# A decoder kernel in which couplings move from VectorE to ScalarE, the router's pick goes by logits, and one scan and one decay stand earlier

## What is computed

```
x = norm(x + random_features(x))
x = norm(x + attention(x, ctx))
# three cycles: gf = sigmoid(net3(mean of x)), once; tf = sigmoid(net4(out)), per row
coupling = 0.1 + adaptive_range * (0.7 * gf + 0.3 * tf - 0.5) * 2.0
out = out + coupling * twist(out)          # x = norm(x + out)
# state space: h = a_t * h + x_conv**2, 16 states of each of 512 channels, summed over the states
x = norm(x + mamba(x))
x = norm(x + gelu(x @ ctx.T) * (x @ ctx.T) @ ctx)
probs = softmax(xt @ router_w + router_b)
gate, idx = max(probs), argmax(probs)      # the first of equal ones
x = norm(x + gate * (expert idx of 8)(x))
```

## Time and profile before

| | us |
|---|---|
| median of 3 runs | 3107.59 (3103.23 to 3112.39) |
| the profiled execution | 3099.29 |
| its span | 3097.5 |
| PE busy | 2540.1 (82%) |
| DVE busy | 2495.3 (81%) |
| ACT busy | 1727.8 (56%) |
| POOL busy | 1487.4 (48%) |

### The profile page before, as it was taken

The page is one execution under the profiler, slowest core; times in us unless marked ns, Lnnn a source line. Parts: engine busy times, 40 slices in busy tenths (PEclk is TensorE's granted clock), DMA queues, the critical chain, the costliest instruction groups (busy, mean ns, idle before and its releaser), DMA issues.

```text
span 3097.5 us, 41602 instructions
## 1 busy us (share of the span) xinstructions
PE 2540.1 (82%) x11020; PEld 1469.9 (47%) x11020; DVE 2495.3 (81%) x4288; ACT 1727.8 (56%) x3062; POOL 1487.4 (48%) x1159
## 2 busy tenths in 40 slices
PE   6896888979888897888988788888888889887556
PEld 3544554544444454445545444554544445454323
DVE  2368888897978889898888978788897888978783
ACT  1457564646657474665646466564656646465620
POOL 1046354554535455563545545354553545456460
PEclk7868888888989989999898899898898989978687
DMA  3000000000000000000000000000000000000000
GB/s 131 10 8 10 14 11 14 17 14 7 10 21 10 14 17 14 7 10 21 10 14 13 18 7 10 21 10 14 13 3 21 10 14 7 7 7 1 14 7 7
DMA packets 16849, 45.72 MB, mean 15 GB/s; under 512 B 2248, under 2 KB 7056, under 8 KB 16400
## 3 DMA queue, kind: packets, MB, share of 16 engines
q1 hardware_dynamic: 16656, 43.96, 4.2%
HBM read 35.57 MB, written 8.39 MB: 14 GB/s over the span
## 4 chain that ended last, share of the span: by engine, by line
PE 47%; DVE 28%; issue 14%; ACT 7%; DVEq 2%; POOL 1%; ACTq 0%; DMA 0%; SPq 0%; POOLq 0%
PE bank L535 45%; DVE h_ring L1087 14%; DVE x L1199 3%; DVE ln_stats L387 2%; DVE smax L991 1%; POOL ysum L1671 1%; ACT a_ring L1479 1%; DVE x L405 1%; DVE xpad L1093 1%; PE bank L413 1%; DVE soft L1066 1%; ACT L1485 1%; ACT L1339 1%; DVE ln_mv L391 1%; ACT spare L1420 1%
## 5 line engine op out<-in xcount | busy, mean ns | idle before, releaser
L1671 POOL TENSOR_TENSOR ysum<-ysum,h_ring 128x512 f32<-128x512 f32 x896 | 1155.2, 1289 | 633.3 <-DVE h_ring L1087 571.3
L1087 DVE TENSOR_TENSOR_SCAN h_ring<-a_ring,bank 128x512 f32<-128x512 f32 x1024 | 1172.7, 1200 | 27.2 <-ACT bank L1474 16.2
L1479 ACT ACTIVATE a_ring<-soft,decay 128x510 f32<-128x510 f32 x1024 | 675.7, 717 | 198.4 <-DVE h_ring L1087 198.0
L535 PE MATMUL bank<-w_expert_w,x45T 128*128 128x512 f32 x1024 | 541.1, 675 | 199.0 <-DVE x L1199 191.4
L535 PEld LDWEIGHTS bank<-w_expert_w,x45T 128*128 128x128 f32 x1024 | 213.2, 216 | 490.9 <-DVE x L1199 253.5
L1658 POOL TENSOR_TENSOR soft<-xc,soft 128x512 f32<-128x512 f32 x64 | 81.0, 1276 | 655.2 <-ACT soft L1457 655.2
L535 PE MATMUL bank<-x3T,w_winT 128*128 128x512 f32 x512 | 291.0, 704 | 39.7 <-ACT x3T L419 31.4
L991 DVE TENSOR_REDUCE smax<-bank 128x4 f32<-128x480 f32 x256 | 156.4, 652 | 143.1 <-PE bank L535 143.1
L535 PE MATMUL bank<-qT,kmask 32*120 32x256 f32 x1024 | 207.2, 497 | 50.2 <-ACT spare L1386 40.6
L535 PE MATMUL bank<-spare,w_cn_w 128*128 128x256 f32 x768 | 217.7, 408 | 37.0 <-ACT spare L1416 22.4
L1199 DVE SCALAR_TENSOR_TENSOR x<-bank,weight,x 128x256 f32<-128x256 f32 x512 | 212.5, 474 | 40.4 <-PE bank L535 40.4
(11 more groups left out here) (149 smaller groups left out, 3890.2 us busy)
## 6 DMA issues: line engine op xcount, KB each, us to landing
x0T<-in_xT SPq DMA_DIRECT2D x16, 512.0 KB, 3.3
x<-in_x SPq DMA_DIRECT2D x16, 512.0 KB, 4.3
out<-x SPq DMA_DIRECT2D x16, 512.0 KB, 3.0
ctxT<-in_ctxT SPq DMA_DIRECT2D x16, 240.0 KB, 2.5
ctxTb<-in_ctxT SPq DMA_DIRECT2D x16, 240.0 KB, 2.7
ctxb<-in_ctx SPq DMA_DIRECT2D x16, 240.0 KB, 3.0
w_expert_w<-in_expert_w SPq DMA_DIRECT2D x1, 2048.0 KB
w_winT<-in_winT SPq DMA_DIRECT2D x1, 1024.0 KB
```

The lines of the kernel that those rows point to most:

```text
L535: return pe.matmul(o, l, r, start=start, stop=stop)
L1087: scanned.then(v.tensor_tensor_scan(h_ring[:, k % HRING, :], a_ring[:, k % RING, :, :].rearrange("p b s -> p (b s)"), xc2, 0.0, ALU.mult, ...
L1479: a.activation(a_ring[:, k % RING, :, 1:S], delta[:, c, :].rearrange("p (b s) -> p b s", b=NB)[:, :, 1:S], ACT.Exp, scale=decay[:, k:k + 1 ...
L1671: p.tensor_tensor(out=total, in0=first, in1=h_ring[:, k % HRING, :], op=ALU.add)\
```

## The change

Three things. The coupling is made on ACT, as an Identity activation with the gate scale as scale and the base as bias, right behind the gate's tanh, and the base likewise on ACT behind the global network's tanh; DVE's `rotate` waits for the coupling. The expert is picked from the logits less their maximum (those equal to 0), in `route`, ahead of the exponential, and the weight is the reciprocal of the sum alone, since the largest term is 1. And in the order of the first cycle DVE's `states(m, 32)` becomes 33 and ACT's `decays(m, 36)` becomes 37, with the third square placed at k = 36 instead of 38.

```diff
-SQUARE_AT = (0, 18, 38, 59)
+SQUARE_AT = (0, 18, 36, 59)
...
-            def global_base(g):
-                v.wait_ge(glob_ready.sem, glob_ready.at(g, 3))
-                v.tensor_scalar(base[:, :], gt[:, :], glob_scale[:, :], base_sign[:, :], ALU.mult, ALU.add)\
-                    .then_inc(base_ready.sem, 1)
-                cyc_chain.start(v, g)
...
                 if s == 0:
-                    v.wait_ge(base_ready.sem, base_ready.at(g, 1))
-                v.wait_ge(gate_ready.sem, gate_ready.at(g, s + 1))
-                cyc_chain.link(v.tensor_scalar(couple[:, b, :], gate[:, b, :], gate_scale[:, :], base[:, b:b + 1],
-                                               ALU.mult, ALU.add))
+                    cyc_chain.start(v, g)
+                v.wait_ge(couple_ready.sem, couple_ready.at(g, s + 1))
...
+                v.wait_ge(logit_ready.sem, logit_ready.at(g, 1))
+                pick_chain.start(v, g)
+                pick_chain.link(v.scalar_tensor_tensor(out=prank[:, :, :], in0=logit[:, :, :], scalar=0.0,
+                                                       in1=over_tiles(row("rank")), op0=ALU.is_equal, op1=ALU.mult))
+                pick_chain.link(v.tensor_reduce(rmax[:, :], prank[:, :, :], AX, ALU.max))
+                pick_chain.then(v.tensor_tensor(out=pick[:, :, :], in0=prank[:, :, :], in1=over_experts(rmax[:, :]),
+                                                op=ALU.is_equal))
+
+            def weigh_expert(g):
+
                 v.wait_ge(prob_ready.sem, prob_ready.at(g, 1))
-                pick_chain.start(v, g)
-                pick_chain.then(v.tensor_reduce(pmax[:, :], prob[:, :, :], AX, ALU.max))
                 pick_chain.link(v.tensor_reduce(psm[:, :], prob[:, :, :], AX, ALU.add))
-                pick_chain.then(v.reciprocal(pinv[:, :], psm[:, :]))
-                pick_chain.link(v.tensor_tensor(out=pick[:, :, :], in0=prob[:, :, :], in1=over_experts(pmax[:, :]),
-                                                op=ALU.is_equal))
-                pick_chain.then(v.tensor_tensor(out=pgate[:, :], in0=pmax[:, :], in1=pinv[:, :], op=ALU.mult))
-                pick_chain.link(v.tensor_tensor(out=prank[:, :, :], in0=pick[:, :, :], in1=over_tiles(row("rank")),
-                                                op=ALU.mult))
-                pick_chain.link(v.tensor_reduce(rmax[:, :], prank[:, :, :], AX, ALU.max))
-                pick_chain.link(v.tensor_tensor(out=pick[:, :, :], in0=prank[:, :, :], in1=over_experts(rmax[:, :]),
-                                                op=ALU.is_equal))
+                pick_chain.link(v.reciprocal(pinv[:, :], psm[:, :]))
                 pick_chain.end()
-                v.tensor_tensor(out=weight[:, :, :], in0=pick[:, :, :], in1=over_experts(pgate[:, :]),
+                v.tensor_tensor(out=weight[:, :, :], in0=pick[:, :, :], in1=over_experts(pinv[:, :]),
                                 op=ALU.mult).then_inc(weight_ready.sem, 1)
...
-                states(m, 32)
-                if f is not None:
-                    global_base(f)
+                states(m, 33)
+                if f is not None:
                     rotate(f, 0)
                     rotate(f, 1)
                 states(m, 34)
...
+                    a.wait_ge(glob_ready.sem, glob_ready.at(g, 3))
+                    a.activation(base[:, :], gt[:, :], ACT.Identity, bias=base_sign[:, :], scale=glob_scale[:, :])\
+                        .then_inc(base_ready.sem, 1)
...
                     a.activation(gate[:, b, :], bank[b][:, 0:S], ACT.Tanh, bias=half_b4[:, :], scale=0.5)\
                         .then_inc(gate_ready.sem, 1)
+                    if s == 0:
+                        a.wait_ge(base_ready.sem, base_ready.at(g, 1))
+                    a.wait_ge(gate_ready.sem, gate_ready.at(g, s + 1))
+                    a.activation(couple[:, b, :], gate[:, b, :], ACT.Identity, bias=base[:, b:b + 1],
+                                 scale=gate_scale[:, :]).then_inc(couple_ready.sem, 1)
...
-                decays(m, 36)
+                decays(m, 37)
                 if f is not None:
                     cycle(f, 0)
                     nat()
```

More of the change, by code:

```diff
@@ L245, in program @@
         prob = sb("prob", [P, NT, EXPERTS])
-        pmax = sb("pmax", [P, NT])
         psm = sb("psm", [P, NT])
         pinv = sb("pinv", [P, NT])
-        pgate = sb("pgate", [P, NT])
         pick = sb("pick", [P, NT, EXPERTS])
@@ L337, in program @@
         gate_ready = sem("gate_ready", CYC)
-        cyc_chain = chain("cyc_chain", 3 * CYC)
+        couple_ready = sem("couple_ready", CYC)
+        cyc_chain = chain("cyc_chain", 2 * CYC)
         z_ready = sem("z_ready", 2 * CYC)
@@ L364, in program @@
         prob_ready = sem("prob_ready", 1)
-        pick_chain = chain("pick_chain", 8)
+        pick_chain = chain("pick_chain", 5)
         weight_ready = sem("weight_ready", 1)
@@ L1154, in route @@
                                 op=ALU.subtract).then_inc(logit_ready.sem, 1)
-            def pick_expert(g):
+                v.wait_ge(logit_ready.sem, logit_ready.at(g, 1))
[6 more added lines that the diff above has]
+            def weigh_expert(g):
                 v.wait_ge(prob_ready.sem, prob_ready.at(g, 1))
-                pick_chain.start(v, g)
-                pick_chain.then(v.tensor_reduce(pmax[:, :], prob[:, :, :], AX, ALU.max))
                 pick_chain.link(v.tensor_reduce(psm[:, :], prob[:, :, :], AX, ALU.add))
-                pick_chain.then(v.reciprocal(pinv[:, :], psm[:, :]))
-                pick_chain.link(v.tensor_tensor(out=pick[:, :, :], in0=prob[:, :, :], in1=over_experts(pmax[:, :]),
-                                                op=ALU.is_equal))
-                pick_chain.then(v.tensor_tensor(out=pgate[:, :], in0=pmax[:, :], in1=pinv[:, :], op=ALU.mult))
-                pick_chain.link(v.tensor_tensor(out=prank[:, :, :], in0=pick[:, :, :], in1=over_tiles(row("rank")),
-                                                op=ALU.mult))
-                pick_chain.link(v.tensor_reduce(rmax[:, :], prank[:, :, :], AX, ALU.max))
-                pick_chain.link(v.tensor_tensor(out=pick[:, :, :], in0=prank[:, :, :], in1=over_experts(rmax[:, :]),
-                                                op=ALU.is_equal))
+                pick_chain.link(v.reciprocal(pinv[:, :], psm[:, :]))
                 pick_chain.end()
-                v.tensor_tensor(out=weight[:, :, :], in0=pick[:, :, :], in1=over_experts(pgate[:, :]),
+                v.tensor_tensor(out=weight[:, :, :], in0=pick[:, :, :], in1=over_experts(pinv[:, :]),
                                 op=ALU.mult).then_inc(weight_ready.sem, 1)
@@ L1256, in turn_ @@
                 if b is not None:
-                    pick_expert(b)
+                    weigh_expert(b)
                 states(m, 22)
```

## The result

| | before | after |
|---|---|---|
| median of the runs, us | 3109.05 (4 runs) | 3176.39 (4 runs, 3167.32 to 3200.83) |
| ratio to before | | 1.0254, 95% interval 1.0223 to 1.0284 |
| span of the profiled execution | 3097.5 | 3176.4 |
| DVE busy | 2495.3 | 2418.8 |
| ACT busy | 1727.8 | 1787.0 |

DVE has 76 us less to do, and the kernel takes 67 us more by the medians and 79 us by the profiled spans. The forecast was 3212, with a range of 3172 to 3240. The sign and the place were right; the size of two terms was not, one in each direction. The ratios in this document and their intervals are the ones on record; they are not the quotients of the medians beside them (here 1.0217) and differ from these by up to 0.4%.

A forecast was written before the change was run, and what follows sets the result against it. No one engine bounds all; the path runs from ACT's table load through the network and PE's experts to DVE's combine. 13 turns at 7.4 us (96) plus other turns sum to +104, on 3107.6 giving 3212 us, range 3172 to 3240.

The forecast's parts named there:

- The hold: ACT waits for DVE's scan of step 33 before the third square, so the gelu table load starts 7.68 us later.
- The chain behind it: From the gelu table's end on ACT to the first gate: 5.49 us at full clock instead of 6.25, a gain of 0.76.
- TensorE's clock: PE idles between layers 1 and 2, so layers 2 to 4 run at the lower clock: 1.46 us more.
- Who waits: Experts 4 and 5 on PE end 8.38 us later; one combine goes ahead (0.39), so DVE's combine comes 8.0 later.
- The couplings: Moved from DVE to ACT, six a turn: only the second pair of rotations gains, 0.45 us in a turn.
- DVE's wait for the square goes under the wait for the experts: DVE's 0.88 us wait for ACT's square goes, but is hidden under its wait for PE's experts.
- The pick: DVE gains about 2 us in expert picking, but PE is late behind it: only 0.19 a turn comes through.
- The rest: Turns outside the 13 loop turns: turn 1 adds 3.5 us, turn 15 5.5, the last two -1, turn 0 no hold.
- Rival 2: Only DVE's own path counts, as if the experts were in time: 3184 or 3165 us; chance 0.07.
- Rival 1: PE's clock stays up, or comes back before it matters: 3192 us; chance 0.2.
- Rival 4: Faster, without ACT's hold: DVE's savings are left, 3098 or 3031 us; chance 0.03 faster, 0.03 for the edge.
- 3: Rival: low clock also covers keys and experts, and `route` delays the softmax: +2 us a turn, 3238; chance 0.08.

## Why the prediction held, and where it failed

*The hold:* predicted 7.68 later for the table load, measured 7.66. The step is right, in its place and in its size, and so is the reading of the plan (step 33). ACT's idle time is 6.44 for "about 6.4".

*The chain behind it:* 5.49 at full clock predicted; 5.50 with PE kept busy. Right.

*TensorE's clock:* this term was mis-sized. I took 1.46 from turn 1, where PE idles 7.03 us ahead of the same matmuls; measured are 2.54. I had read the granted clock of turn 1 from 271 to 276 only and took what the matmuls lost there for the price of the whole chain. Turn 1 of the kernel before, and turn 8 after (the granted clock is the third number from the end):

```profile
269.89:276.72 6.83, 3.45 (x8) 2.82 (x9) 6.83 (x8) 4.51 (x8) 6.05 (x6) 0.50 0.00 0
276.72:279.48 2.76, 2.50 (x10) 1.47 (x10) 1.20 (x2) 1.82 (x4) 2.47 (x3) 1.00 0.00 0
```

```profile
1560.65:1570.89 10.24, 7.16 (x18) 4.82 (x18) 0.00 (x0) 6.35 (x15) 2.52 (x2) 0.50 0.00 0
```

In turn 1 the clock was back after 3.45 of the 6.21 us of these matmuls. Here it stays low for 6.85 of the 7.64 us from layer 2's start to layer 4's end (1564.04 to 1571.68, for 5.03 before). Why it comes back later here isn't shown; the chains differ, as in the first cycle the global network's small matmuls stand between the layers. My upper end of 1.8 was too low too.

*Who waits:* the combine's shift was to be 8.0; the fourth stretch is 9.04 longer, which is 8.0 and the clock's 1.08 more. One product ahead of the others (0.4) is as predicted, and so is PE, not DVE's own path, as what is late. DVE's idle time ahead of the first rotation was to be 8 to 10 and is 12.22 in turn 8: my own numbers give 10.6 (1511.74 to 1521.28 + 1.05), and the rest is the clock's higher price.

*The couplings:* 0.45 in the second pair, nothing in the first and the third: measured -0.45 in the fifth stretch. Right in the changed kernel. One instruction takes 0.60 on ACT instead of the 0.55 I took. But the step "DVE's wait for the square goes under the wait for the experts" holds only with the square moved; without that the couplings cost 0.78. That is the cover that I named and didn't price.

*The pick:* this step failed. I predicted that 0.19 of about 2 us comes through, since PE idled only 0.19 us for DVE in turn 8, and I had turn 8 stand for all. Turn 9 of the same profile of the kernel before:

```profile
1666.73 0.60 PE L783 MATMUL bank<-w_ident,weight 128*8 128x128 f32 x4
1671.15 6.19 PE L535 MATMUL bank<-w_wo,qT 128*128 128x256 f32 x16 [3.81 <-DVE qT L1014]
```

PE idles 3.81 us for DVE there and the product behind it runs at the lower clock, 6.19 for 3.72. In ten of the 13 loop turns that idle time is 1.77 us or more; in three, turn 8 among them, it is about 0.2. In the changed kernel ten of 13 have none. The third stretch of turn 8 and that of turn 10, as rows of a stretch, say what sets turn 8 apart:

```profile
1472.27:1493.70 21.43, 21.24 (x116) 11.44 (x109) 19.84 (x34) 12.99 (x24) 16.20 (x13) 0.70 0.00 1
1840.32:1861.78 21.46, 15.17 (x108) 9.11 (x109) 19.76 (x34) 12.87 (x24) 16.22 (x13) 1.00 0.00 1
```

Both are as long. In turn 8 TensorE had the lower clock for much of the stretch, was busy nearly throughout and so as late as DVE; in turn 10, at the full clock, it idled 3.81 us for DVE. The three turns with 0.2 of idle time are those with a granted clock of 0.70 to 0.72. In the changed kernel a stretch at 0.70 or 0.71 takes 20.9 to 21.0 us, the two at 1.00 take 18.87: the same pick gives 0.5 where TensorE is slow and 2.6 where it isn't. DVE's own saving, from the logits to the scan behind the weights, is 2.2 in the mean (5.6 for 7.8), near the "about 2" of the prediction; what failed is how much of it PE would hide. So the saving comes through: 2.0 in a turn, of which 0.6 is the three products that ran at the lower clock before and don't after, and 19 us between the medians with the pick alone.

*The rest:* turn 15 was to add 5.5 and takes 0.7 off. Its hold is there (ACT idles 6.12 us for DVE's scan, and from norm 2's copies on ACT to the combine of experts 4 and 5 it is 26.5 for 19.9); what makes the rest of that turn 7.3 shorter I didn't work out. The last two turns give 3.9 for the 1 taken; turns 0 and 1 add 4.1 for 3.5. By the sum: 9.04 - 0.45 - 2.00 - 0.48 (small stretches) = 6.11 for my 7.4, and the median ended 36 below the forecast, near the low end. The terms make 25 of that (79 for 104); the other 10 is the scale, as the profiled execution lay 8.3 below its median before and 1.8 above it after. Too small a clock term hid part of the error in the pick. That the time lies in the range is in part luck. Rival 2 (only DVE's own path), at 3184 the nearest in its number, is false: the combine waits for PE's experts. Rival 1 (the clock stays up), at 3192, is false too: layers 2 to 4 run at the lower clock. Rival 4 is false; 3 was right in that the low clock costs more, but keys and experts take as long as before (1.78 and 3.60).

## What to carry to other kernels

Before an instruction is moved ahead of a block on an in-order engine, read what it waits for, and when that comes: here one square and one decay, 1.3 us of work, held the network for 7.7 us in every turn and made the kernel 2.5% slower than before; with the same piece behind the block it is about 1% faster than before, which is about what the pick gives alone. Count an idle time over all turns before one turn stands for them, above all where TensorE's clock differs between turns: an engine at half its clock hides another's lateness. A saving on one engine is worth what is late behind it, and moved work pushes back what stands behind it on its new engine: with the old schedule the couplings took 0.45 us off DVE in one stretch and made another 0.78 longer, by a later square.

## What the runs showed of the hardware

- The price of PE's idle time. Behind 6.84 us without a matmul, layer 2 took 2.08 us for 1.13; with matmuls of no use in that gap it took 1.13. The Trainium skill ("TensorE: Matmul & The Clock Gate", Part 1) has activity release the throttle; this pair of rows agrees.
- The same kernel, profiled twice, had turns of 178.68 and 180.41 us in the mean. The fourth and the fifth stretch agree within 0.01 us; the third and the last are 0.35 and 1.50 longer in the second profile, with 3.6 to 3.8 us more at the lower clock in each. Its two medians, 3057 and 3072, lie 15 us apart, on two chips.
- A tiny instruction of DVE with two SBUF inputs can last until POOL's instruction ends. The old comparison (L1162, 128x32) took 1.23 to 1.26 us in all 13 loop turns, and each time a POOL instruction of 1.26 us had started 0.06 to 0.09 us ahead of it; in the last turn, with none beside it, it took 0.16. In turn 8:

```profile
1475.45 2.65 POOL L1671 TENSOR_TENSOR ysum<-ysum,h_ring 128x512 f32<-128x512 f32 x2
```

```profile
1475.52 1.25 DVE L1162 TENSOR_TENSOR pick<-prob,pmax 128x32 f32<-128x32 f32 x1
```

  In that turn the reduction ahead of it, with one input, took 0.16 with POOL at work. After the change the product with the rank takes 192 ns in the median (1317 at most) and the comparison behind it 927; the old comparison took 1245:

```profile
L1148 DVE SCALAR_TENSOR_TENSOR prank<-logit,w_rows x16: 191/192/1317, 391.3 to 3121.6; 128x32 f32<-128x32 f32 x16
L1151 DVE TENSOR_TENSOR pick<-prank,rmax x16: 192/927/976, 391.8 to 3122.0; 128x32 f32<-128x32 f32 x16
```
